# A graph network on one core: target rows copied into PSUM by ScalarE in the edge stages, and stationary weights in the first mixture of experts

## The chip, the cores and the metric

The kernel runs on one core of a Trainium2 chip, as one program. The metric is the time on the device in microseconds (us), lower is better. TensorE does matmuls, VectorE and ScalarE work on SBUF and PSUM, GpSimd here does little but issue indirect DMAs (gathers and scatters by index), and SyncE issues the other DMAs.

## The reference, cut to what matters

Four layers are computed over 625 nodes with 768 features. Only the first one is touched by the change. It is a graph layer over 20000 edges (source, target), and behind it a mixture of eight experts of which each token takes two.

```python
def gatv2(x, src, dst, Ws, bs, Wd, bd, attn):            # called twice: 8 heads of 96, 1 head of 768
    fs = (x @ Ws + bs).reshape(-1, H, D)
    fd = (x @ Wd + bd).reshape(-1, H, D)
    e = jax.nn.leaky_relu(fs[src] + fd[dst], 0.2)
    logits = jnp.einsum('ehd,hd->eh', e, attn)
    m = jax.ops.segment_max(logits, dst, num_segments=N)
    ex = jnp.exp(logits - m[dst])
    ...
    out = jax.ops.segment_sum(alpha[:, :, None] * fs[src], dst, num_segments=N)
# mixture: two experts of eight per token, E = 8, D = 768, F = 3072
#   y = gelu(x @ w1[e] + b1[e]) @ w2[e] + b2[e], mixed by the gates
```

## The kernel before, in words

**Two edge stages.** Two tables of 625 rows (776 floats each: 768 features and 8 linear terms) are written to HBM, one for source nodes and one for target nodes. The 20000 edges are 157 tiles of 128. For each tile GpSimd issues a gather of 128 source rows (L538), a gather of 128 target rows (L541) and, six tiles behind, a scatter of the tile's logits (L549). All go in this one order on GpSimd, and a scatter starts only when the scatter before it has landed (`s_sc`). There are eight buffers for each table's rows. VectorE does the arithmetic: it adds the two rows (L1254, 776 columns), takes the maximum with zero and multiplies by the attention vector (first stage L1258; second stage L1268, which sums as well), in the first stage sums each head (L1263), and finishes the logit (L1275). In the first stage it also makes two one-hot rows of 626 bf16 columns for each tile (L1206), with which TensorE counts edges into PSUM banks 0 to 6 (L611), and SyncE clears two tables in HBM beside it, one transfer behind every third scatter. ScalarE has nothing to do in either stage. GpSimd's order and these waits set the pace:

```python
for i in range(ET + LAG):          # ET = 157 tiles, LAG = 6
    if i < ET:
        gathers(i)                 # L538, L541
    ...
    if i >= LAG:
        scatter(i - LAG, g)        # L549: waits s_lg (logits ready) and s_sc (last scatter landed)
```

**The first mixture** works on units of 256 token slots, each with one expert's weights, 8 units here. A unit has 12 groups `g` of 256 hidden features. Fp32 accuracy comes from fp32r matmuls of a rounded part and a rest: every product is three matmuls, (high, high), (high, low), (low, high). `first(u, g)` makes the hidden features from weights as the stationary operand and token columns as the moving one; it has 36 matmuls of `columns` columns. `second(u, g)` makes the output with tokens stationary and weights moving; it has 12 matmuls of 384 columns for each 128 tokens, into banks 4 to 7. Both are at L780. `columns` is 128, 192 or 256, by how far the unit is filled (`empty`). TensorE's order is first(g + 1), second(g), then the next unit's rows are transposed (`turn`, L773), second(11) and the next unit's first(0), behind which stands the branch of the unit loop. ScalarE rounds weights (L1038, L1043) and applies Gelu (L1050); VectorE makes the rests of the weights (L1555, L1560), splits the hidden features (L1566, L1568), and copies the output out of PSUM (L1585) when second(11) is done, from where GpSimd stores it (L584).

## Time and profile before

| | |
|---|---|
| time, median of 3 runs | 4110.46 us (4107.86 to 4110.98) |
| the profiled execution's own time | 4104.76 us |
| its span | 4103.0 us |
| TensorE, weight loads, VectorE, ScalarE, GpSimd busy | 60%, 49%, 53%, 19%, 28% |
| mean granted TensorE clock | 0.763 of full speed |

The times come from the device; the profile is one execution, taken apart by engine. In it a line such as L549 is a line of the kernel. A group of instructions has its busy time and the mean of one. A timeline row has the start, the duration, the engine and, in brackets, how long the engine was idle before it and what ended that. A window row has its ends and length, the busy time of PE, PEld (weight loads), DVE, ACT and POOL, with the number of instructions as (x...), then the granted TensorE clock as a share of full speed, the DMA share and GB/s.

### The profile page before, as it was taken

To read this page: it belongs to the slowest core of one execution; us is meant where nothing else is said; L and a number is where in the kernel's file an instruction comes from. 1 tells how busy PE (TensorE), PEld (TensorE's weight loads), DVE (VectorE), ACT (ScalarE), POOL (GpSimd) and SP (SyncE) were. 2 spreads that over 40 slices of the span, in tenths; PEclk is the share of its full clock that TensorE was granted. 3 is DMA by queue.
4 is the path that set the end of the run, shared out by engine and by line. 5 is a ranking of instruction groups with operands and counts; after the bars stand their busy time and mean duration, and the time that the engine had idled before them with its cause. 6 is when DMAs were issued, how large, how long until landed. Compare 5 with 4: busy or idle time off the path is not lost.

```text
span 4103.0 us, 37498 instructions
## 1 busy us (share of the span) xinstructions
PE 2477.2 (60%) x13152; PEld 2028.0 (49%) x13153; DVE 2179.4 (53%) x3944; ACT 769.6 (19%) x1107; POOL 1132.9 (28%) x987
## 2 busy tenths in 40 slices
PE   8445555556600000015599888888588487886899
PEld 4333343345300000003599888888275244475799
DVE  3666677767444444434575455545474524567332
ACT  0000000024000000001364334433072111044110
POOL 0667677730277777750100000000100000000000
PEclk9666655667855555556799999999788687998799
DMA  8666666653365666640675555554300001100111
GB/s 261 198 206 212 213 178 178 172 136 115 99 174 173 176 177 178 179 116 1 196 265 194 171 177 177 179 170 148 114 1 12 10 27 36 58 12 24 70 70 42
DMA packets 117558, 543.01 MB, mean 132 GB/s; under 512 B 31195, under 2 KB 31451, under 8 KB 112220
## 3 DMA queue, kind: packets, MB, share of 16 engines
q0 software_dynamic: 65920, 264.29, 22.1%
q1 hardware_dynamic: 50088, 262.32, 19.0%
q10 hardware_dynamic: 1386, 14.06, 1.1%
q8 instruction: 121, 1.98, 0.2%
q14 instruction: 43, 0.35, 0.0%
HBM read 486.31 MB, written 54.26 MB: 132 GB/s over the span
## 4 chain that ended last, share of the span: by engine, by line
PE 43%; issue 31%; POOL 9%; DMA 8%; DVE 8%; ACT 1%; SPq 0%; POOLq 0%; DVEq 0%; ACTq 0%
PE PS L780 18%; PE PS L642 7%; PE PS L873 6%; DMA logits<-lgr,key 6%; PE PS L697 4%; POOL logits L549 3%; POOL WB L538 3%; POOL WB L541 2%; PE PS L683 1%; PE PS L750 1%; PE PS L854 1%; PE PS L740 1%; DVE stats L1181 1%; PE PS L626 1%; DVE W L1343 1%
## 5 line engine op out<-in xcount | busy, mean ns | idle before, releaser
L611 PE MATMUL PS<-O 128*125 128x512 bf16 (+9 forms) x1727 | 404.9, 410 | 355.5 <-DVE O L1206 344.3
L683 PE MATMUL PS<-ident,W 125*125 125x125 f32 x650 | 113.7, 313 | 811.7 <-issue 737.8
L1254 DVE TENSOR_TENSOR WB<-WB 128x776 f32<-128x776 f32 x276 | 267.4, 969 | 561.9 <-DMA WB<-dst_rows,idx 558.4
L611 PEld LDWEIGHTS PS<-O 128*125 128x125 bf16 x1727 | 275.3, 200 | 485.2 <-DVE O L1206 404.5
L683 PEld LDWEIGHTS PS<-ident,W 125*125 125x125 f32 x650 | 96.1, 215 | 827.0 <-issue 771.9
L780 PE MATMUL PS<-urowsT,w1s 128*128 128x192 f32 (+2 forms) x3492 | 430.4, 283 | 73.2 <-issue 65.6
L549 POOL DMA_INDIRECT logits<-lgr,key x314 | 416.3, 1326 | 210.9 <-DMA logits<-lgr,key 118.8
L780 PEld LDWEIGHTS PS<-urowsT,w1s 128*128 128x128 f32 x3492 | 428.4, 199 | 75.5 <-issue 71.1
L538 POOL DMA_INDIRECT WB<-src_rows,idx x314 | 321.2, 1023 | 293.8 <-DMA dst_rows<-O 198.7
L642 PE MATMUL PS<-WB,XT 128*125 128x384 f32 (+1 forms) x1120 | 377.5, 500 | 13.8 <-DMA WB<-in_L_gnn_Wos 12.6
L780 PE MATMUL PS<-w2s,hid 128*128 128x384 f32 x2016 | 369.0, 336 | 5.3 <-issue 5.3
L780 PEld LDWEIGHTS PS<-w2s,hid 128*128 128x128 f32 x2016 | 346.5, 188 | 6.1 <-issue 6.1
L541 POOL DMA_INDIRECT WB<-dst_rows,idx x276 | 309.2, 1120 | 84.7 <-issue 74.9
L531 POOL TENSOR_TENSOR rstd<-var,mhalf 125x5 f32<-125x5 f32 x13 | 15.3, 1174 | 1117.9 <-DVE var L1186 1071.5
L697 PE MATMUL PS<-F,PT 125*125 125x96 f32 (+3 forms) x1500 | 294.2, 349 | 9.8 <-DVE O L1367 9.5
L642 PEld LDWEIGHTS PS<-WB,XT 128*125 128x125 f32 x1120 | 210.7, 189 | 177.3 <-issue 30.6
L999 ACT ACTIVATE W<-W,nmx 125x625 f32<-125x625 f32 x130 | 106.1, 816 | 881.0 <-DVE nmx L1345 878.1
L873 PE MATMUL PS<-w3s,XT 128*128 128x384 f32 x1440 | 255.4, 340 | 11.1 <-DVE w3s L1617 11.1
L873 PEld LDWEIGHTS PS<-w3s,XT 128*128 128x128 f32 x1440 | 255.1, 190 | 12.3 <-issue 12.2
L697 PEld LDWEIGHTS PS<-F,PT 125*125 125x125 f32 x1500 | 232.5, 204 | 51.4 <-issue 16.2
L584 POOL DMA_DIRECT2D slot_outs<-F x8 | 5.8, 729 | 871.7 <-DVE F L1585 871.7
L1560 DVE TENSOR_TENSOR w2s<-PB,w2s 128x1536 fp32r<-128x1536 f32 x97 | 170.4, 1757 | 132.6 <-ACT w2s L1043 132.6
(224 smaller groups left out, 3186.8 us busy)
## 6 DMA issues: line engine op xcount, KB each, us to landing
XN<-in_L_ffn_w SPq DMA_DIRECT2D x98, 769.0 KB, 4.4
PB<-in_L_ffn_w SPq DMA_DIRECT2D x97, 768.0 KB, 5.0
logits<-NEG ACTq DMA_DIRECT2D x9, 1367.2 KB
WB<-logits SPq DMA_DIRECT2D x5, 2187.5 KB
slot_rows<-NEG SPq DMA_DIRECT2D x13, 768.0 KB
slot_outs<-NEG SPq DMA_DIRECT2D x12, 768.0 KB
C<-in_L_ffn_expert_w SPq DMA_DIRECT2D x8, 1152.0 KB, 5.5
NEG<-in_L_ffn_expert_w SPq DMA_DIRECT2D x8, 1152.0 KB, 6.5
```

The source lines that it names most:

```text
L538: pool.indirect_dma_start(out=gs[u], out_offset=None, in_=src_rows, in_offset=bass.IndirectOffsetOnAxis(ap=idx[:, i, 0:1], axis=0)).then_i ...
L541: pool.indirect_dma_start(out=gd[u], out_offset=None, in_=dst_rows, in_offset=bass.IndirectOffsetOnAxis(ap=idx[:, i, 1:2], axis=0)).then_i ...
L549: pool.indirect_dma_start(out=tables[g], out_offset=bass.IndirectOffsetOnAxis(ap=key[:, i:i + 1], axis=0), in_=lgr[:, i % EU, 0:HEADS[g][" ...
L611: mm = pe.matmul(PSz[0:R, a:b], oh[:, slot, 1, c * R:(c + 1) * R], oh[:, slot, 0, a - c * N:b - c * N], start=(first and fresh), stop=last ...
L642: mm = pe.matmul(PS[0:R, 4 + g % 4, 0:hw], XT[:, k, t * R:(t + 1) * R], w[:, k, half * hw:(half + 1) * hw], start=(k == 0), stop=(k == kc ...
L683: tr = pe.transpose(PSz[0:R, 1024 * (1 + s % 2) + b * P:1024 * (1 + s % 2) + b * P + R], src[:, b * R:(b + 1) * R], ident[0:R, 0:R])
L697: mm = pe.matmul(PS[0:R, bank, 0:cw], PT[0:R, s % 2, b, :], F[0:R, b, col:col + cw], start=(b == 0), stop=(b == T - 1))
L780: mm = pe.matmul(out, w(i), x(j), start=first and n == 0, stop=last and n == 2)
L873: mm = pe.matmul(PS[:, 4 + 2 * ((MB3 + d) % 2) + half, 0:384], XT2[:, a, k, t * R:t * R + P], w3s[:, 2 * u + k // 3, b, col:col + 384], st ...
L999: act.activation(W[0:R, v % 4, :], W[0:R, v % 4, :], ACT.Exp, bias=nmx[:, v % 4:v % 4 + 1], accum_out=den[:, v % 4:v % 4 + 1]).then_inc(s_ ...
L1254: dve.tensor_tensor(gs[u], gs[u], gd[u], ALU.add).then_inc(s_z, 1)
L1560: dve.tensor_tensor(w2s[:, g % 2, 1, :], uw2[g % 2], w2s[:, g % 2, 0, :].bitcast(F32), ALU.subtract).then_inc(s_lo2, 1)
```

## The change

In the edge stages ScalarE copies the target rows into PSUM, so that VectorE adds SBUF and PSUM. In the first stage PSUM has one bank free (bank 7), so the row goes in two halves of 384 columns through `zh`; in the second stage whole rows go through four areas `zw`. The source one-hot is made by ScalarE in two activations (Abs of the gap, Relu of one minus it).

```diff
+        zh = PS[:, 7, 0:D // 2]
+        zw = [PSz[:, 1024 * b:1024 * b + GW] for b in range(4)]
...
+            def edges(g):
...
+                def half_copy(i, u, half):
+                    wait(act, s_mul, 2 * i + half)
+                    act.copy(zh, gd[u][:, half * (D // 2):(half + 1) * (D // 2)]).then_inc(s_gc, 1)
...
+                def step(i, u, rounds):
+                    gathered(u, rounds)
+                    if g == 0:
+                        half_copy(i, u, 0)
+                        node_gaps(i)
+                        half_copy(i, u, 1)
+                        source_onehot(i, u)
+                    else:
+                        wait(act, s_lg, ET + i - 3)
+                        act.copy(zw[u % 4], gd[u]).then_inc(s_gc, 1)
...
-                def add(i, u, rounds):
-
-                    dve.wait_ge(s_gat[u], rounds + 32 * (ER + (u < ET % EU)) * g + 32)
-                    dve.tensor_tensor(gs[u], gs[u], gd[u], ALU.add).then_inc(s_z, 1)
-
-                def product(i, u):
-                    dve.wait_ge(s_z, i + 1)
-                    dve.scalar_tensor_tensor(out=gs[u][:, 0:D], in0=gs[u][:, 0:D], scalar=0.0, in1=attn, op0=ALU.max,
-                                             op1=ALU.mult).then_inc(s_mul, 1)
+                def half_product(i, u, half):
+                    part = slice(half * (D // 2), (half + 1) * (D // 2))
+                    dve.wait_ge(s_gc, 2 * i + half + 1)
+                    dve.tensor_tensor(zh, gs[u][:, part], zh, ALU.add).then_inc(s_z, 1)
+                    dve.wait_ge(s_z, 2 * i + half + 1)
+                    dve.scalar_tensor_tensor(out=gs[u][:, part], in0=zh, scalar=0.0, in1=attn[:, part],
+                                             op0=ALU.max, op1=ALU.mult).then_inc(s_mul, 1)
...
+                def add(i, u):
+                    dve.wait_ge(s_gc, 2 * ET + i + 1)
+                    dve.tensor_tensor(zw[u % 4], gs[u], zw[u % 4], ALU.add).then_inc(s_z, 1)
```

VectorE, first edge stage, one tile. Before:

```order
L1275 SCALAR_TENSOR_TENSOR lgr<-dots,WB 128x8
L1254 TENSOR_TENSOR WB<-WB 128x776
L1257 REGISTER_ALU
L1258 SCALAR_TENSOR_TENSOR WB<-WB,PB 128x768
L1206 ISA
L1206 TENSOR_SCALAR O<-XT,idf 128x626
L1263 TENSOR_REDUCE dots<-WB 128x8
L1206 ISA
L1206 TENSOR_SCALAR O<-XT,idf 128x626
```

and with the change (the lines are those of the changed kernel; L1338 is the add, L1340 the product, L1345 the add of the linear terms):

```order
L1338 TENSOR_TENSOR PS<-WB,PS 128x384
L1340 SCALAR_TENSOR_TENSOR WB<-PS,PB 128x384
L1291 ISA
L1291 TENSOR_SCALAR O<-XT,idf 128x626
L1337 REGISTER_ALU
L1338 TENSOR_TENSOR PS<-WB,PS 128x384
L1340 SCALAR_TENSOR_TENSOR WB<-PS,PB 128x384
L1345 TENSOR_TENSOR WB<-WB 128x8
L1349 TENSOR_REDUCE dots<-WB 128x8
```

One one-hot and the wide add are gone, the add and the product stand twice at half the width, and the second half stands behind a copy of ScalarE.

In the mixture the high and low parts of the moving operand go through one matmul (`both`, two runs of `columns` side by side in a bank), so each high weight tile is loaded once. `second` has the weights stationary too and the hidden features moving, so the output comes out transposed, in banks 2 to 7, and is turned back by TensorE (`turn_back`) at the unit's end. The small part, in the second half of a bank, is added by ScalarE and VectorE: ScalarE copies it out with the bias, VectorE adds the large part, ScalarE applies Gelu.

```diff
-                def three(out, w, x, first, last):
-
-                    for n, (i, j) in enumerate(((0, 0), (0, 1), (1, 0))):
-                        mm = pe.matmul(out, w(i), x(j), start=first and n == 0, stop=last and n == 2)
-                    return mm
+                def both(bank, columns):
+
+                    return PS[:, bank, :].rearrange("p (j n) -> p j n", j=2)[:, :, 0:columns]
...
+                            pe.matmul(both(q % 2, columns), w1s[:, g % 2, 0, w:w + P],
+                                      urowsT2[:, :, k * TU:k * TU + columns], start=k == 0, stop=False)
+                            mm = pe.matmul(PS[:, q % 2, 0:columns], w1s[:, g % 2, 1, w:w + P],
+                                           urowsT2[:, 0, k * TU:k * TU + columns], start=False, stop=k == KD - 1)
...
+                    for c in range(FC):
+                        pe.wait_ge(s_hl, (u * NG + g) * FC + c + 1)
+                        for k in range(KD):
+                            w = c * D + k * P
+                            pe.matmul(both(2 + k, columns), w2s[:, g % 2, 0, w:w + P],
+                                      hid2[:, g % 2, :, c * TU:c * TU + columns],
+                                      start=g == 0 and c == 0, stop=False)
+                            mm = pe.matmul(PS[:, 2 + k, 0:columns], w2s[:, g % 2, 1, w:w + P],
+                                           hid2[:, g % 2, 0, c * TU:c * TU + columns],
+                                           start=False, stop=g == NG - 1 and c == FC - 1)
...
                     for g in range(NG - 1):
                         first(u, g + 1, columns)
-                        second(u, g, -(-columns // P))
-                    turn(u + 1)
+                        second(u, g, columns)
+                    turn(u + 1, (0, 1))
+                    second(u, NG - 1, columns)
...
+                    turn(u + 1, (2,))
                     first(u + 1, 0)
+                    turn_back(u)
...
+                def sum_hidden(u, g):
+                    for c in range(FC):
+                        q = g * FC + c
+                        part = hid[:, g % 2, c * TU:(c + 1) * TU]
+                        dve.wait_ge(s_un, u * (NG * FC) + q + 1)
+                        dve.tensor_tensor(part, PS[:, q % 2, 0:TU], part, ALU.add).then_inc(s_ha, 1)
```

TensorE, one group of a unit with 192 columns. Before (first, then second):

```order
L780 MATMUL PS<-urowsT,w1s 128x192 x36
L780 MATMUL PS<-w2s,hid 128x384 x24
```

and with the change, for a unit with 128 columns, the last pair of first and the first two pairs of second (`first` has 12 such pairs, `second` too; w1s and w2s are the weights):

```order
L808 MATMUL PS<-urowsT,w1s 128x2x128
L810 MATMUL PS<-urowsT,w1s 128x128
L823 MATMUL PS<-hid,w2s 128x2x128
L826 MATMUL PS<-hid,w2s 128x128
L823 MATMUL PS<-hid,w2s 128x2x128
L826 MATMUL PS<-hid,w2s 128x128
```

A group goes from 60 matmuls (48 in a unit of 128 columns) to 48, and both halves of it now depend on `columns`.

## Rows read from the trace of the kernel before

**Rows 1.** Windows: both edge stages, a unit of 128 columns, a later unit
```profile
108.00:880.00 772.00, 404.87 (x1727) 275.31 (x1727) 539.58 (x946) 4.09 (x2) 547.94 (x471) 0.63 0.62 188
1096.00:1834.00 738.00, 0.15 (x2) 0.16 (x1) 306.69 (x640) 1.08 (x3) 539.73 (x471) 0.50 0.60 172
...
2085.00:2162.00 77.00, 75.19 (x588) 74.87 (x588) 59.05 (x66) 46.80 (x51) 0.80 (x1) 1.00 0.79 268
...
2292.00:2409.00 117.00, 105.28 (x732) 105.01 (x732) 59.99 (x65) 46.84 (x51) 0.71 (x1) 0.95 0.53 176
```

**Rows 2.** Windows of the scatters alone (L549)
```profile
130.00:525.00 395.00, 95.94 (x79) 0.65 0.66 208
525.00:878.00 353.00, 106.46 (x79) 0.62 0.57 164
1121.00:1820.00 699.00, 212.31 (x156) 0.50 0.60 172
```

**Rows 3.** Second edge stage: the scatters' group
```profile
L549 POOL DMA_INDIRECT logits<-lgr,key x157 | 213.3, 1358 | 84.7 <-DMA logits<-lgr,key 41.4 <-issue 29.6 <-DVE lgr L1275 13.7
```

**Rows 4.** Second edge stage: timeline of GpSimd and VectorE
```profile
1443.08 0.97 DVE L1254 TENSOR_TENSOR WB<-WB 128x776 f32<-128x776 f32 x1 [2.00 <-DMA WB<-dst_rows,idx]
1443.44 1.42 POOL L541 DMA_INDIRECT WB<-dst_rows,idx  x1 [0.30 <-DMA logits<-lgr,key]
...
1445.17 0.99 POOL L549 DMA_INDIRECT logits<-lgr,key  x1 [0.30 <-DVE lgr L1275]
...
1449.60 1.45 POOL L549 DMA_INDIRECT logits<-lgr,key  x1 [0.92 <-DMA logits<-lgr,key]
...
1472.03 0.98 POOL L549 DMA_INDIRECT logits<-lgr,key  x1 [0.80 <-DMA logits<-lgr,key]
...
1475.85 1.67 POOL L549 DMA_INDIRECT logits<-lgr,key  x1 [0.30 <-issue]
```

**Rows 5.** First edge stage: timeline, a sum per head beside a scatter
```profile
606.80 0.94 DVE L1263 TENSOR_REDUCE dots<-WB 128x8 f32<-128x768 f32 x1
606.85 0.99 POOL L549 DMA_INDIRECT logits<-lgr,key  x1 [0.30 <-issue]
```

**Rows 6.** Groups of VectorE and ScalarE that price the new instructions
```profile
L1263 DVE TENSOR_REDUCE dots<-WB 128x8 f32<-128x768 f32 x157 | 148.0, 943 | 0.0
...
L1235 DVE TENSOR_TENSOR O<-PS,PB 125x384 f32<-125x384 f32 x20 | 11.1, 557 | 46.1 <-PE PS L642 46.1
...
L1555 DVE TENSOR_TENSOR w1s<-XN,w1s 128x1536 fp32r<-128x1536 f32 x98 | 171.6, 1751 | 0.0
L1050 ACT ACTIVATE F<-PS,b1c 128x256 f32<-128x256 f32 x192 | 91.0, 474 | 305.6 <-PE PS L780 305.6
L1568 DVE TENSOR_TENSOR hid<-F,hid 128x512 fp32r<-128x512 f32 x96 | 66.5, 693 | 3.3
```

**Rows 7.** Mixture: timeline, a hand-over from ScalarE to VectorE
```profile
2379.65 1.48 ACT L1043 CAST w2s<-PB 128x1536 fp32r<-128x1536 f32 x1 [2.32 <-PE PS L780]
2381.16 1.76 DVE L1560 TENSOR_TENSOR w2s<-PB,w2s 128x1536 fp32r<-128x1536 f32 x1 [1.88 <-ACT w2s L1043]
```

**Rows 8.** Mixture: groups of TensorE by shape
```profile
L780 PE MATMUL PS<-w2s,hid 128*128 128x384 f32 x2016 | 369.0, 336 | 5.3 <-issue 5.3
L780 PE MATMUL PS<-urowsT,w1s 128*128 128x192 f32 x1584 | 194.4, 283 | 42.1 <-issue 42.1
...
L780 PE MATMUL PS<-urowsT,w1s 128*128 128x256 f32 x1116 | 145.4, 291 | 31.1 <-issue 23.5 <-DVE w1s L1555 3.9 <-DVE urowsT L1548 3.7
...
L780 PE MATMUL PS<-urowsT,w1s 128*128 128x128 f32 x792 | 90.9, 274 | 0.0
```

**Rows 9.** Mixture: timeline at the end of a unit, and of the last one
```profile
2393.43 4.48 PE L780 MATMUL PS<-urowsT,w1s 128*128 128x256 f32 x36
...
2409.87 3.52 PE L780 MATMUL PS<-urowsT,w1s 128*128 128x192 f32 x15 [11.97 <-issue]
...
2858.52 1.82 DVE L1585 COPY F<-PS 128x768 f32<-128x768 f32 x2 [1.83 <-PE PS L780]
```

More of the change, by code:

```diff
@@ L801, in second, with turn_back @@
                         wait(pe, s_uy, u * SU)
[L802 to L810 removed]
+                    for c in range(FC):
[8 more added lines that the diff above has]
+                                           start=False, stop=g == NG - 1 and c == FC - 1)
+                    mm.then_inc(s_ub, 1)
+                def turn_back(u):
+                    for half in range(2):
+                        pe.wait_ge(s_ya, u * 2 + half + 1)
+                        for s in range(SU):
+                            for k in range(KD // 2):
+                                tr = pe.transpose(PS[:, 2 + 3 * half + s, k * P:(k + 1) * P],
+                                                  yT[:, half * (KD // 2) + k, s * P:(s + 1) * P], ident[:])
+                        tr.then_inc(s_yt, 1)
                 def groups(u, columns):
@@ L825, in unit @@
                         groups(u, TU // 2)
-                        second(u, NG - 1, SU // 2)
                     with pe.Else():
@@ L1049, in hidden, with output_part @@
                         act.wait_ge(s_ua, u * (NG * FC) + q + 1)
-                        act.activation(hid[:, g % 2, c * TU:(c + 1) * TU], PS[:, q % 4, 0:TU], ACT.Gelu,
-                                       bias=b1c[:, g % 2, c:c + 1]).then_inc(s_ug, 1)
+                        act.activation(hid[:, g % 2, c * TU:(c + 1) * TU], PS[:, q % 2, TU:2 * TU], ACT.Identity,
+                                       bias=b1c[:, g % 2, c:c + 1]).then_inc(s_un, 1)
+                def hidden(u, g):
+                    for c in range(FC):
+                        part = hid[:, g % 2, c * TU:(c + 1) * TU]
+                        act.wait_ge(s_ha, u * (NG * FC) + g * FC + c + 1)
+                        act.activation(part, part, ACT.Gelu).then_inc(s_ug, 1)
+                def output_part(u):
+                    act.wait_ge(s_ub, u * NG + NG)
+                    for half in range(2):
+                        wait(act, s_yt, u * 2 + half - 1)
+                        act.copy(yT[:, 3 * half:3 * half + 3, :], PS[:, 2 + 3 * half:5 + 3 * half, TU:2 * TU])\
+                           .then_inc(s_yb, 1)
                 def unit(u):
                     for g in range(NG):
+                        if g:
+                            small_part(u, g)
                         hidden(u, g)
@@ L1290, in step @@
                     else:
+                        add(i, u)
                         if lag:
@@ L1596, in mixture0 @@
                         unit(u)
-                dve.wait_ge(s_ua, units * (NG * FC) + FC)
+                dve.wait_ge(s_yt, units * 2)
                 dve.nop().then_inc(s_left, 1)
```

157 lines of the change are left out of this document (99 added, 58 removed).

## The prediction, made before the changed kernel was run

> **What bounds the kernel now.** I read the windows of the stages first, because the change touches two kinds of stage with different limits. The two edge stages take 772 and 738 us, the mixture's units 77 us each where they have 128 columns and about 117 us otherwise [rows 1]. In the second edge stage TensorE and ScalarE do nothing, VectorE is busy 307 of 738 us and GpSimd 540. So the chain there is GpSimd's: two gathers and a scatter a tile. The windows of the scatters give the pace: 156 scatters in 699 us are 4.48 us a tile in the second stage; in the first, 79 in 395 us are 5.00 us while SyncE clears tables, and 79 in 353 us are 4.47 us after that [rows 2].
>
> Next I looked at what makes GpSimd's own instructions long. The scatters of the second stage take 1.36 us on the mean [rows 3], but 0.99 where nothing disturbs them [rows 4]. In the timeline, a gather that started at 1443.44, while VectorE's add of two SBUF rows (from 1443.08 to 1444.05) ran, took 1.42 us and ended 0.81 us after that add [rows 4]. The 1.45 and the 1.67 in the same rows are of that kind too. So an issue that comes while VectorE reads two SBUF rows waits for the end of that. A head sum that ran beside a scatter, with one SBUF input, left it at 0.99 [rows 5]. The page "SBUF — State Buffer" of the Trainium skill, section "Who interferes with whom", has this as a rule: a VectorE instruction with two SBUF inputs keeps a GpSimd instruction that reads SBUF waiting, one with a single SBUF input outside the two-port modes does not. By that rule, which the 1.42 and the 0.99 bear out, the changed add and product disturb nobody.
>
> What is left without the stretch? Two undisturbed scatters, each followed by two undisturbed gathers, show the next scatter 4.43 us behind (1445.17 to 1449.60, the last one having waited 0.92 for the landing of the one before) and 3.82 us behind (1472.03 to 1475.85, no wait) [rows 4]. The lower one is GpSimd's pure issue time, the upper one is set by the scatter's way through the DMA queue behind two gathers.
>
> In the mixture TensorE bounds: 105 of 117 us are busy, and 12 us are one hole behind the next unit's first group, ended by nothing that the profile shows, where the unit's branch stands [rows 1, 9]. The kernel before has its matmuls at 0.130 us each for 256 columns (145.4 / 1116), 0.123 for 192, 0.115 for 128 and 0.183 for 384 [rows 8]. From 128 to 192 columns nothing is gained or lost, so there the weight load sets the pace, and above it the columns do. The counts say which units there are: 1584 matmuls of 192 columns are 4 units (11 groups of 36), 792 of 128 are 2, and the remaining 2 are full.
>
> **Second edge stage.** ScalarE's copy of 776 columns (about 0.85 us, between 0.47 for 256 and 1.48 for 1536 [rows 6, 7]) lies beside GpSimd's 4 us and four areas let it run ahead: nothing. VectorE's add and product stay at 0.97 and 0.95. GpSimd's tile goes from 4.48 to between 3.82 and 4.43. I take the middle, 4.12, as the DMA queue still has the same bytes: 0.36 x 156 = **56 us** gained (ends 8 and 103).
>
> **First edge stage.** VectorE now has a chain with ScalarE in it, since both halves go through one bank. A half is add and product at 384 columns with PSUM: 0.557 each by the nearest row [rows 6]. Two SBUF rows, 0.693 for 512 columns and 1.751 for 1536, give 1.033 ns a column and 0.164 fixed [rows 6]; at that slope the PSUM row has 0.557 - 0.397 = 0.160 fixed: no price for PSUM. "VectorE: DVE Perf Modes" of the Trainium skill, section "The TRN2 errata", gives 120 cycles of fixed cost for PSUM sources against 58 for SBUF, which would add about 0.06 us to each of four, 0.26 us a tile, and bring the stage's gain to about nothing; the rows disagree with it, and the sum goes by them. Between the halves stands ScalarE's copy of 384 columns, 0.57 (0.474 for 256, and 0.78 ns a column more [rows 6, 7]); the target one-hot lies beside it. The chain is 4 x 0.557 + 0.57 + head sum 0.94 + two small ones at 0.16 = 4.06, and some five hand-overs at 0.03 (2381.13 to 2381.16 [rows 7]) = 4.2 us. The copy of the next tile's first half lies beside the head sum. ScalarE has two copies and two activations of 626 columns, about 2.7 us, and TensorE's counting waits for nobody longer than before. So VectorE at 4.2 and GpSimd at 4.12 are about even, and I take 4.25. After the clearing: 0.22 x 79 = 17 us. During it, one scatter in three waits for SyncE's transfer, which the change leaves; of the others' stretch I count 0.2 x 79 = 15 us. Together **32 us** gained (ends: 84 gained with 3.9 us a tile after the clearing and 4.5 during it; 50 lost if the hand-overs are 0.2 each, 5.06 us a tile).
>
> **Mixture, groups.** The slope from 256 to 384 columns gives 0.236 for 512. A group half is 12 pairs: 12 x (0.236 + 0.130) = 4.39 us in a full unit, against 36 x 0.130 = 4.69 for first and 24 x 0.183 = 4.39 for second; 12 x (0.183 + 0.123) = 3.67 with 192 columns, against 4.42 and 4.39; 12 x (0.130 + 0.115) = 2.94 with 128, against 4.13 and 2.20. With 11 firsts and 12 seconds: a 192 unit gains 8.2 + 8.6 = 16.9, a full one 3.3, and each one 0.3 for the next unit's first(0).
>
> VectorE gets more in each group: rests of both weights 1.75 + 1.76 [rows 6, 7], two sums of 256 columns from PSUM at 0.42, four smaller splits, 1.42; with the wait for Gelu (0.47) and for ScalarE's rounding behind it, I make it 6.4 to 6.5 us a group, whatever the columns. That is below the 7.3 us of a 192 group, but above the 5.9 of a 128 group: the two small units become VectorE's, 12 x 6.5 = 78 us and some 5 for the unit's end, against 77 now: 12 us lost in the two.
>
> **Mixture, unit ends.** The third pair of row blocks is now turned only behind second(11), and then ScalarE (0.59) and VectorE (0.68, by the 512-column row [rows 6]) have to pass before the next first(0): 1.4 us of idle TensorE. turn_back is 12 transposes, 1.5 us. The hole of 12 us stays, as the branch does [rows 9]. So 2.9 us lost a unit: 192 units net 14.3 x 4 = 57, full ones 0.7 x 2 = 1. After the last unit the output was copied out right behind second(11) [rows 9]; now first(8, 0) (4.4), the turned rows and the turning back stand ahead: 7 us lost on the path. Larger memsets ahead of the mixture lie before the wait for scattered token rows: nothing (3 us if that cover were gone). Sum of the mixture: 57 + 1 - 12 - 7 = **39 us** gained (ends: 75 gained if small units stay TensorE's and unit ends cost nothing, 20 lost if the longer chain shows in each group).
>
> **The sum.** 56 + 32 + 39 = 127. The profiled execution took 4104.8 us, 5.7 below the median, so it would take 3978; against the median, 3983. I say 3980.
>
> **The rivals.** (a) *The issue stays stretched*, because the stretch hangs on the product or on fp32 work as such and not on a second SBUF input. For it speaks that no row shows GpSimd beside an instruction that reads PSUM; against it the 1.42 beside an add and the 0.99 beside a head sum [rows 4, 5]. Both edge stages then gain nothing: 4110 - 39 = 4071. The Trainium skill leans to it in one place: the same section of "SBUF — State Buffer" infers that making descriptors needs only the write side, so that an add of two SBUF rows would not hold it up. Chance 0.09. (b) *The landing gives way too.* Without stretches the queue runs evenly and tiles go at 3.85: 42 us more in the second stage, and with small units at 77 another 12 or so: 3925. Rows that wait 0.8 to 0.9 for landings speak against it. Chance 0.13. (c) *The mixture's longer chain shows.* PSUM, Gelu and sums go round ScalarE, VectorE, ScalarE, VectorE in each group, with weights rounded in between; at 8 us a group the mixture gains nothing: 4022 to 4045. Chance 0.10. (d) *Slower: the first edge stage becomes a ping-pong of two engines.* Its one bank makes ScalarE and VectorE wait for each other six times a tile. The chain is 4.06 us without hand-overs, and the stage's tile now takes (395 + 353) / 158 = 4.73 [rows 2]. It eats the 95 us of the other two when a tile costs 0.6 more, 5.3 us, that is with hand-overs of 0.25 us and more. At 6 us a tile it loses 200: 4110 - 95 + 200 = 4215. For it: the order on ScalarE puts an activation between the copies. Against: 0.03 in the row. Chance 0.05.
>
> **How the numbers follow.** The forecast has 0.63, from 3950 to 4020 by its own ends. A measurement of this kernel tells about 0.2%, 8 us, from no change. To hold 8 in 10, the range takes (b)'s middle and most of (c): 3925 to 4055, leaving out (a), (d) and the outer part of (b). Faster by over 0.2%: all but (d) and a rest, 0.94; within it 0.02; slower 0.04.
>
> **What would show it.** Scatters and gathers near 0.99 and 0.95 us, 4.1 us a tile in the second stage and 4.2 to 4.3 in the first; VectorE's adds near 0.56; pairs of matmuls that sum to 0.31 us with 192 columns, units of 192 near 103 us, of 128 near 83; the hole of 12 us at each unit's end. Scatters still at 1.36 say (a), idle VectorE behind ScalarE's copies says (d), idle TensorE inside groups says (c).

## The result, and the profile after

The changed kernel takes **3962.91 us** (median of 4 runs, 3955.41 to 3966.71), the kernel before in the same comparison 4109.16 (4101.91 to 4110.98): a ratio of **0.9645, 95% interval 0.9626 to 0.9664**. A second comparison gave 3961.46 against 4105.06, 0.9650 (0.9632 to 0.9667). So 146 us went (predicted: 130), and the predicted 3980 is 17 us too high. The copy of the change in that second comparison had a span of 3955.4 us in its trace, 10 us under the one read here.

| | before | after | predicted gain | gain |
|---|---|---|---|---|
| profiled span, us | 4103.0 | 3965.0 | 127 | 138 |
| first edge stage, start of the first gather to start of the last scatter | 769.1 | 715.1 | 32 | 54 |
| second edge stage | 718.8 | 666.2 | 56 | 53 |
| mixture, first transpose of rows to the next layer's norm | 895.7 | 865.9 | 39 | 30 |
| the rest | 1719.4 | 1717.8 | 0 | 2 |

(The rest is the span less the three rows above.) That the sum came near is in part luck: two terms were off in opposite directions, by 22 and by 9 us. The windows of the changed kernel, of the first and the second edge stage, of a unit with 192 columns, a full one and a small one (span, then busy time and count of TensorE, weight loads, VectorE, ScalarE, GpSimd, then the granted clock, DMA share and GB/s):

```profile
109.00:824.50 715.50, 371.25 (x1727) 256.32 (x1727) 569.39 (x1260) 391.74 (x631) 457.87 (x471) 0.69 0.66 203
1050.00:1716.00 666.00, 0.00 (x0) 0.00 (x0) 299.26 (x628) 127.01 (x157) 454.25 (x471) 0.50 0.66 188
2080.30:2183.40 103.10, 89.33 (x601) 87.86 (x601) 72.90 (x116) 57.24 (x77) 0.72 (x1) 0.93 0.63 215
2183.40:2303.00 119.60, 106.14 (x600) 92.05 (x600) 72.82 (x115) 57.46 (x77) 0.71 (x1) 0.96 0.50 173
1901.50:1984.70 83.20, 75.31 (x589) 72.92 (x589) 71.73 (x115) 55.68 (x79) 0.00 (x0) 0.95 0.67 229
```

Against [rows 1], GpSimd is busy for 458 instead of 548 us in the first stage and for 454 instead of 540 in the second, for the same 471 instructions. A 192-column unit fell from about 117 to 103 us, the two small ones rose from 78.4 and 77.1 to 83.1 and 82.5, and a full one rose from 117.3 to 119.6. The windows of the scatters alone, during the clearing, after it, and in the second stage:

```profile
126.00:520.00 394.00, 81.65 (x81) 0.65 0.67 215
520.00:824.00 304.00, 74.95 (x75) 0.75 0.64 184
1068.00:1716.00 648.00, 153.18 (x157) 0.50 0.65 185
```

That is 4.86, 4.05 and 4.13 us a tile, where [rows 2] has 5.00, 4.47 and 4.48. And the groups of the second edge stage's GpSimd instructions (scatter, gather of source rows, gather of target rows), where [rows 3] has 1358 ns for the scatter:

```profile
L562 POOL DMA_INDIRECT logits<-lgr,key x157 | 154.7, 985 | 113.4 <-DMA logits<-lgr,key 79.8 <-issue 31.7 <-DVE lgr L1368 1.9
L551 POOL DMA_INDIRECT WB<-src_rows,idx x157 | 152.2, 969 | 157.3 <-DMA dst_rows<-O 109.8 <-issue 47.5
L554 POOL DMA_INDIRECT WB<-dst_rows,idx x138 | 130.5, 946 | 44.5 <-issue 40.5 <-DMA logits<-lgr,key 4.0
```

No instruction of this stage is stretched any more (0.99 us at most once the pipeline is full, where 131 of 457 took more than 1.05 before), and the largest wait before the scatter is now the landing of the scatter before it (79.8 us; 41.4 before). The timeline of GpSimd and VectorE answers to [rows 4]:

```profile
1438.86 0.97 DVE L1354 TENSOR_TENSOR PS<-WB,PS 128x776 f32<-128x776 f32 x1 [1.78 <-ACT PS L1020]
1439.64 0.99 POOL L562 DMA_INDIRECT logits<-lgr,key  x1 [0.30 <-issue]
...
1442.21 0.95 POOL L554 DMA_INDIRECT XT<-dst_rows,idx  x1 [0.30 <-issue]
1443.46 0.99 POOL L562 DMA_INDIRECT logits<-lgr,key  x1 [0.31 <-issue]
...
1443.46 0.97 DVE L1354 TENSOR_TENSOR PS<-WB,PS 128x776 f32<-128x776 f32 x1 [2.69 <-ACT PS L1020]
...
1447.90 0.99 POOL L562 DMA_INDIRECT logits<-lgr,key  x1 [0.92 <-DMA logits<-lgr,key]
```

At 1443.46 an add and a scatter start together, and the scatter takes its 0.99 us. From there to the scatter at 1447.90 are 4.44 us, 0.92 of them a wait for the landing; the one before came 3.82 us apart, with no wait. These are the prediction's two ends.

### The profile page after: what moved, and what is told of

It reads as the page before. It is cut to its first block, busy times and chain, and to the rows that moved or that the text cites. A ratio compares the mean times of both kernels' runs of the same rounds, so it can differ in the third digit from the quotient of the medians.

```text
span 3965.0 us, 39470 instructions
## 1 busy us (share of the span) xinstructions
PE 2387.2 (60%) x12372; PEld 1917.4 (48%) x12373; DVE 2312.3 (58%) x4660; ACT 1360.7 (34%) x2102; POOL 960.6 (24%) x987
## 4 chain that ended last, share of the span: by engine, by line
PE 40%; issue 30%; DMA 11%; DVE 11%; POOL 4%; ACT 3%; DVEq 0%; SPq 0%; POOLq 0%; ACTq 0%
PE PS L656 8%; DMA logits<-lgr,key 7%; PE PS L903 6%; PE PS L808 5%; PE PS L823 4%; PE PS L711 4%; PE PS L810 2%; DMA WB<-dst_rows,idx 2%; PE PS L826 2%; POOL WB L551 1%; PE PS L697 1%; POOL logits L562 1%; PE PS L764 1%; DVE w1s L1645 1%; PE PS L884 1%
## 5 line engine op out<-in xcount | busy, mean ns | idle before, releaser
L808 PE MATMUL PS<-urowsT,w1s 128*128 128x384 f32 (+2 forms) x1164 | 375.7, 386 | 85.1 <-issue 64.3
L562 POOL DMA_INDIRECT logits<-lgr,key x314 | 313.7, 999 | 273.8 <-DMA logits<-lgr,key 196.0
L1354 DVE TENSOR_TENSOR PS<-WB,PS 128x776 f32<-128x776 f32 x157 | 152.4, 971 | 358.4 <-ACT PS L1020 358.4
L823 PE MATMUL PS<-hid,w2s 128*128 128x384 f32 (+2 forms) x1152 | 338.8, 362 | 0.5 <-DVE hid L1668 0.5
L810 PE MATMUL PS<-urowsT,w1s 128*128 128x192 f32 (+2 forms) x1164 | 306.1, 263 | 0.0
L1020 ACT COPY PS<-WB 128x776 f32<-128x776 f32 x138 | 111.6, 809 | 561.3 <-DMA WB<-dst_rows,idx 561.3
L826 PE MATMUL PS<-hid,w2s 128*128 128x192 f32 (+2 forms) x1152 | 288.9, 251 | 0.0
L808 PEld LDWEIGHTS PS<-urowsT,w1s 128*128 128x128 f32 x1164 | 232.2, 200 | 109.4 <-issue 82.0
L1000 ACT COPY PS<-WB 128x384 f32<-128x384 f32 x276 | 133.2, 483 | 358.4 <-DMA WB<-dst_rows,idx 263.3
L1338 DVE TENSOR_TENSOR PS<-WB,PS 128x384 f32<-128x384 f32 x314 | 176.2, 561 | 135.5 <-ACT PS L1000 134.4
```

The lines of the kernel that those rows point to most:

```text
L562: pool.indirect_dma_start(out=tables[g], out_offset=bass.IndirectOffsetOnAxis(ap=key[:, i:i + 1], axis=0), in_=lgr[:, i % EU, 0:HEADS[g][" ...
L808: pe.matmul(both(q % 2, columns), w1s[:, g % 2, 0, w:w + P], urowsT2[:, :, k * TU:k * TU + columns], start=k == 0, stop=False)
L810: mm = pe.matmul(PS[:, q % 2, 0:columns], w1s[:, g % 2, 1, w:w + P], urowsT2[:, 0, k * TU:k * TU + columns], start=False, stop=k == KD - 1)
L823: pe.matmul(both(2 + k, columns), w2s[:, g % 2, 0, w:w + P], hid2[:, g % 2, :, c * TU:c * TU + columns], start=g == 0 and c == 0, stop=False)
L826: mm = pe.matmul(PS[:, 2 + k, 0:columns], w2s[:, g % 2, 1, w:w + P], hid2[:, g % 2, 0, c * TU:c * TU + columns], start=False, stop=g == NG ...
```

## The experiments

Twelve runs in four comparisons, each on a chip of its own, with the kernel before beside them (4105.31, 4105.06, 4106.49 and 4105.78 us). First the parts alone, and the two halves of the SBUF question.

**The edges alone.** The change, with the mixture's functions and memsets of the kernel before.

```diff
-                dve.memset(PS[:, 0:2, :], 0.0)
-                link(dve.memset(PS[:, 2:8, :], 0.0))
+                dve.memset(PS[:, 3, 0:TU], 0.0)
+                link(dve.memset(PS[:, 6:8, 0:384], 0.0))
...
-                def both(bank, columns):
+                def three(out, w, x, first, last):
```

> The edge stages of the change with the mixture of before. If the two parts are independent, this keeps what the two edge stages gained in the profile of the change (from the first source gather to the last scatter: 769.1 to 715.0 us and 718.8 to 666.2 us) and nothing else: near 4002 us. If part of the measured gain came from the mixture helping elsewhere (clock, code loading), it would lie outside 3994 to 4012.

Measured: 4059.79, ratio 0.9888 (0.9869 to 0.9907). A miss by 58 us. The second stage gained as it should (671.8 us), but the first took 768.7.

**The mixture alone.** The reverse: the kernel before with the change's mixture.

```diff
-                def three(out, w, x, first, last):
+                def both(bank, columns):
```

> The mixture of the change with the edge stages of before. Independent parts: 4104 - 30 = near 4075 us, units of 192 columns 103 us from one first matmul to the next, small ones 82 us. If the mixture's gain needed the new edge stages, near 4104.

Measured: 4063.96, ratio 0.9898 (0.9879 to 0.9917): 41 us gained, where 30 were forecast. The mixture took 857.3 us in its trace and the 192 units that can be read 100.4 to 102.7, so this copy of it ran 3 to 9 us faster than in the two traces of the change.

**Copies into SBUF.** The four areas of the second stage lie in SBUF, so that the add and the product read two SBUF rows again, and all else stays.

```diff
-        zw = [PSz[:, 1024 * b:1024 * b + GW] for b in range(4)]
+        zw = [XTz[:, (b + 1) * GW:(b + 2) * GW] for b in range(4)]
```

> The change, but in the second edge stage ScalarE copies the target rows into SBUF instead of PSUM; the same copies, waits and order. Theory (a second SBUF input of VectorE holds GpSimd up): scatters back near 1.36 us and a tile near 4.48 us, the stage 50 us longer, the kernel near 4013 us, with the first edge stage as in the change. Rival (the gain comes from ScalarE taking part, from timing, or from the four areas that let VectorE start apart from the gather): scatters stay at 0.99 us, the kernel at 3963 us.

Measured: 4061.38, ratio 0.9896 (0.9875 to 0.9918). The theory's 4013 was missed by 48 us: its first stage too took 769.2 us. The second took 706.7, 35 more than in the edges alone beside it.

**The product from SBUF.** The add reads PSUM but writes its sum to SBUF, so that the product alone has two SBUF inputs.

```diff
-                    dve.tensor_tensor(zw[u % 4], gs[u], zw[u % 4], ALU.add).then_inc(s_z, 1)
+                    dve.tensor_tensor(gs[u], gs[u], zw[u % 4], ALU.add).then_inc(s_z, 1)
...
-                    dve.scalar_tensor_tensor(out=gs[u][:, 0:D], in0=zw[u % 4][:, 0:D], scalar=0.0, in1=attn,
+                    dve.scalar_tensor_tensor(out=gs[u][:, 0:D], in0=gs[u][:, 0:D], scalar=0.0, in1=attn,
```

> The change, but in the second edge stage only the add reads PSUM: it writes its sum to SBUF, and the product reads two SBUF inputs as before. If every VectorE instruction with two SBUF inputs holds GpSimd up for its length, half of the stretch comes back: scatters of 1.15 to 1.25 us, a tile near 4.3 us, the kernel near 3985 us. If the product is what does it all, as most long scatters of before stood beside it: near 4013 us. If it is the add alone: 3963 us.

Measured: 4042.31, ratio 0.9846 (0.9826 to 0.9866). First stage 771.2, second 689.5, 18 more than in the edges alone; without the 56 us of the first stage this is near the 3985 of "half of the stretch".

These three have the first stage of the change line for line, and it took 54 us more than in the change. Where does it stand? In the timeline of the edges alone, TensorE, its weight loads, ScalarE and VectorE:

```profile
706.14 2.90 PE L625 MATMUL PS<-O 128*125 128x512 bf16 x11 [0.92 <-issue]
...
714.19 0.82 ACT L993 ACTIVATE O<-XT,ones 128x626 bf16<-128x626 bf16 x1 [5.11 <-remote]
714.24 0.39 DVE L1257 TENSOR_SCALAR O<-XT,idf 128x626 bf16<-128x626 f16 x1 [5.68 <-remote]
```

ScalarE's and VectorE's one-hots wait for a buffer that TensorE's counting frees. Its matmuls are issued at 706.14, but in the semaphore's records no count comes until 714.1, and from about tile 83 on this happens at every fifth tile: five tiles in 24.5 us instead of 20.4. The question was whether that belongs to these kernels.

**The change again.** No edit.

> The changed kernel, unchanged, once more. Its own trace has 715 us from the first gather of the first edge stage to its last scatter; in the three runs of kernels whose code for that stage is the same (edges alone, SBUF areas, product from SBUF) it took 769 to 771 us, with a stop of 4 us at every fifth tile from tile 83 on, in which VectorE, ScalarE and TensorE all stand. If the stop hangs on something outside the code (the chip or the moment), this run shows it too: about 4018 us. If it belongs to those kernels (where their code or their buffers lie), this run has none: 3963 us, first stage 715 us.

Measured, on a second chip: 3961.46, ratio 0.9650 (0.9632 to 0.9667), first stage 715.5.

**One waiter.** The source one-hot waits behind the target one-hot instead of on TensorE.

```diff
-                    wait(act, s_ohu, i - 1)
+                    act.wait_ge(s_oh, i + 1)
```

> ScalarE's source one-hot no longer waits on the semaphore that TensorE counts up (one-hots used) but on VectorE's target one-hot of the same tile, which has waited on it. If the stops of every fifth tile come from two engines that wait on one semaphore of TensorE, they go: first stage 715 us whatever the run of the unchanged copy beside it shows. If they have another cause, the time is within 8 us of that copy.

Measured: 3963.99, ratio 0.9649 (0.9629 to 0.9669). On this chip the copy had no stops either, so it tells nothing of them.

**The edges alone again**, and **copies into SBUF again**, on a third chip.

> The edges alone once more, unchanged. If the stops of every fifth tile in the first edge stage hang on something outside the code, they are absent or present here as in the other two kernels beside it, whose first stage has the same code: without them 4005 us (first stage 715 us), with them 4060 us (769 us). If they belong to this kernel alone, this run has them and the narrow gather has not.

Measured: 3993.80, ratio 0.9722 (0.9700 to 0.9745), first stage 713.3, second 660.7, mixture 897.8.

> The copies of the second edge stage in SBUF once more, unchanged. First stage as in the two kernels beside it if the stops come from outside the code: then 4004 us without them, of which the second stage's stretched descriptors are 41 us over the change; with them 4061 us.

Measured: 4004.15, ratio 0.9748 (0.9727 to 0.9769), first stage 713.5, second 706.1.

So the stops are not in the code: the same two kernels ran 66 and 57 us faster on the third chip. Whether they hung on the first chip or on the hour, these runs can't tell. The windows of the scatters in the first stage, edges alone on the first chip and on the third:

```profile
560.00:820.00 260.00, 52.25 (x53) 0.68 0.56 164
```

```profile
560.00:820.00 260.00, 64.88 (x65) 0.74 0.64 183
```

Free of the stops, the SBUF pair gives a clear answer: with the copies in SBUF the second stage takes 45 us more than with the copies in PSUM (706.1 against 660.7, same chip), 40 us more than in the trace of the change. Its GpSimd groups, and behind them those of the product from SBUF:

```profile
L562 POOL DMA_INDIRECT logits<-lgr,key x157 | 197.3, 1257 | 78.1 <-issue 47.6 <-DMA logits<-lgr,key 28.2 <-DVE lgr L1368 2.4
L551 POOL DMA_INDIRECT WB<-src_rows,idx x157 | 186.3, 1186 | 157.8 <-DMA dst_rows<-O 110.3 <-issue 47.5
L554 POOL DMA_INDIRECT WB<-dst_rows,idx x138 | 131.1, 950 | 42.4 <-issue 39.9 <-DMA logits<-lgr,key 2.4
```

```profile
L551 POOL DMA_INDIRECT WB<-src_rows,idx x157 | 187.4, 1193 | 157.0 <-DMA dst_rows<-O 109.5 <-issue 47.5
L562 POOL DMA_INDIRECT logits<-lgr,key x156 | 156.0, 1000 | 98.8 <-DMA logits<-lgr,key 60.0 <-issue 35.9 <-DVE lgr L1368 2.9
```

With two SBUF inputs in both, scatter and source gather take 0.27 and 0.22 us more than in the change. With them in the product alone, only the source gather (which falls beside it) is stretched, the scatter is not (1.00 us, where 1.15 to 1.25 were forecast), and the stage costs 18 us more than the edges alone on that chip (689.5 against 671.8). So both of VectorE's instructions, the add and the product, stretch an issue that they meet. That the row is copied and that the work is fp32 play no part, since both stayed. Rival (a) falls. The rule in "SBUF — State Buffer" of the Trainium skill, section "Who interferes with whom", agrees with that. The same section's inference that making descriptors needs only the write side would leave these issues at their length, and they grew by 0.2 us; since they also read their indices from SBUF, the runs don't say which part of an issue waits.

In the first edge stage the copy wasn't moved to SBUF. Its scatters after the clearing fell from 1.33 us on the mean to 1.00, so the same cause is likely there, but only the second stage shows it.

Next, what sets the edge stages now.

**The source one-hot back on VectorE.**

```diff
-                        node_gaps(i)
                         half_copy(i, u, 1)
-                        source_onehot(i, u)
...
+                dve.tensor_scalar(oh[:, slot, 0, :], iota16, idf[:, 0, bass.ds(i, 1)], None, ALU.is_equal)
```

> The source one-hot of the first edge stage goes back to VectorE, and ScalarE only copies. If VectorE sets the tile (its instructions sum to about 3.9 us of 4.1 in the trace of the change), its 0.38 us more come on top: 157 x 0.38 = 60 us over the copy of the change in the same comparison. If the chain over ScalarE (two copies of 0.48 us and two activations of 0.81 us, which stand between the copies) sets it, the copies come sooner and the time is the same or up to 40 us less.

Measured: 3965.84, ratio 0.9656 (0.9638 to 0.9675), 4.4 us over the copy of the change beside it, and not 60; the two intervals overlap. The windows of all engines in the first stage, the copy of the change and this kernel:

```profile
560.00:820.00 260.00, 130.04 (x680) 90.85 (x678) 227.19 (x495) 154.95 (x247) 177.74 (x184) 0.77 0.64 184
```

```profile
560.00:820.00 260.00, 131.31 (x672) 90.36 (x671) 241.62 (x555) 62.33 (x124) 178.96 (x183) 0.76 0.64 184
```

VectorE's busy share went from 87 to 93% and ScalarE's from 60 to 24%, and GpSimd issued as much as before. Neither VectorE nor the chain through ScalarE sets the tile.

**Less traffic.** The gather of the target rows fetches 194 of 776 columns in the second stage.

```diff
-                    out=gd[u], out_offset=None, in_=dst_rows,
+                    out=gd[u] if g == 0 else gd[u][:, 0:194], out_offset=None,
+                    in_=dst_rows if g == 0 else dst_rows.rearrange("n d -> (n d)")[0:N * 194].rearrange("(n d) -> n d", n=N),
...
-                        act.copy(zw[u % 4], gd[u]).then_inc(s_gc, 1)
+                        act.copy(zw[u % 4].rearrange('p (k n) -> p k n', n=194),
+                                 gd[u][:, 0:194].unsqueeze(1).to_broadcast([P, 4, 194])).then_inc(s_gc, 1)
```

> In the second edge stage the gather of the target rows fetches 194 of 776 columns, and ScalarE writes these four times side by side into the same PSUM area, so that every engine has as many instructions of the same size as in the change, and only the traffic falls (from 6.2 to 3.9 KB per edge); the scores of that stage are computed from part of the target row. If the tile (4.15 us in the change) is the scatter's issue until it has landed (3.3 us from its start) and 0.85 us until the next starts, a scatter with less traffic ahead of it lands sooner and the tile falls to what GpSimd's three instructions and their pauses take, 0.97 + 0.95 + 0.99 + 3 x 0.30 = 3.8 us: 157 x 0.35 = 55 us off the second stage, 3908 us. If GpSimd or the chain over VectorE and ScalarE sets it, the second stage stays at 660 to 666 us and the time at 3963 us.

Measured: 3928.34, ratio 0.9560 (0.9538 to 0.9581). The second stage took 609.4 us, 57 less than in the trace of the change (the forecast had 55); the mixture, whose units depend on the scores, had a 192 unit in place of a small one and took 890.3 us instead of 865.0 in the copies into SBUF beside it, so the total isn't comparable (3908 was forecast). The windows of 570 us of scatters of the second stage, in the copy of the change and here, then the scatters' group here:

```profile
1130.00:1700.00 570.00, 136.04 (x138) 0.50 0.66 190
```

```profile
1080.00:1650.00 570.00, 147.92 (x150) 0.50 0.47 128
```

```profile
L563 POOL DMA_INDIRECT logits<-lgr,key x157 | 154.9, 987 | 58.8 <-issue 46.6 <-DMA logits<-lgr,key 10.1 <-DVE lgr L1370 2.2
```

That is 4.13 and 3.80 us a tile. The instructions are the same, the wait before the scatter that a landing ended fell from 79.8 to 10.1 us, and the tile is GpSimd's own time, 2.90 us of issue and three pauses of 0.30. So with full rows the scatter's landing is the limit.

The first stage of this kernel is that of the change, and its trace holds the landings. It settles what sets the pace there, where the profile puts most waits before a scatter down to VectorE's logits (27.3 of 44 us between 560 and 820 us of the change). Of 66 scatters after the clearing (tiles 85 to 150), 49 wait longer than the usual 0.30 us. All 49 start 0.77 to 0.79 us behind the landing of the scatter before, and the logits of such a tile are ready more than 12 us before its scatter. A scatter lands 3.30 us (median) behind its start, and 3.30 + 0.77 = 4.07 us is the tile of that stage (4.10). With the narrow rows the landing comes 2.28 us behind the start, and the next scatter 1.5 us later.

Shortening it at full traffic, with two scatters in flight, wasn't tried: two scatters may write the same row, and their order would be open.

Last, the ends of the units.

**Turn back first.** TensorE turns the output back ahead of the next unit's first product.

```diff
-                    first(u + 1, 0)
                     turn_back(u)
+                    first(u + 1, 0)
```

> At the end of each mixture unit TensorE turns the output of the unit back before it multiplies the first rows of the next unit, where the change does it after. Where the change idles twice there (1.48 us before the next unit's first product and 1.1 to 1.7 us before the turn back), one of the two would be hidden: 8 units x 1.1 to 1.5 = 9 to 12 us under the copy of the change. If VectorE, whose work for the two stands in one order, sets both, the one wait only moves: within 4 us of the copy.

Measured: 3974.93, ratio 0.9681 (0.9666 to 0.9696), so 13.5 us slower than the copy beside it. A miss of both theories, and a premise was wrong: in the change TensorE has no idle time before the turn back. The 1.1 to 1.7 us that the expectation puts there stand before the turn of the third pair of row blocks (L790), at the ends of all units but the full ones, and they stay here. In the change at the end of a 192 unit and of a full one, and then here at the end of the same full one:

```profile
2386.67 0.65 PE L790 MATMUL PS<-ident,F 128*128 128x128 f32 x4 [1.10 <-DVE urowsT L1638]
...
2285.28 0.49 PE L808 MATMUL PS<-urowsT,w1s 128*128 128x512 f32 x1 [1.48 <-DVE urowsT L1638]
```

```profile
2291.23 2.41 PE L837 MATMUL PS<-ident,XT 128*128 128x128 f32 x12 [2.37 <-DVE XT L1675]
2293.29 0.78 PE L808 MATMUL PS<-urowsT,w1s 128*128 128x512 f32 x1
```

The wait for the output's two sums is 2.37 us where that for the turned rows was 1.48; in the change the first product (4.3 us) hides it. Also, the transposes behind the longer gap take 2.41 instead of 1.47 us and the first products 0.78 instead of 0.49. The granted clock is 0.66 in these transposes, and 1.00 in the change's. The longer wait and the transposes come to some 16 us over eight ends; the six holes are 2.5 us shorter in sum (15.1 and 15.8 us before the full units, 8.2 to 8.5 before three 192 units), which leaves 13 us, near the 13.5 between the medians (the two traces lie 19 us apart). Why the holes shift so is open.

**The loop over units written out.** On TensorE alone.

```diff
-                with pe.Fori(1, NU) as u:
-                    with pe.If(u < units):
-                        unit(u)
+                def rest(u):
+                    if u < NU:
+                        with pe.If(units > u):
+                            unit(u)
+                            rest(u + 1)
+
+                rest(1)
```

> TensorE's loop over the mixture units is written out (each further unit inside the condition of the one before), so that its sequencer no longer jumps back between units; the three sizes of a unit and all other engines' loops stay. In the trace of the change the idle time before the first product of a unit in the loop is 5.84, 10.84, 11.99, 10.93, 11.86 and 11.41 us, and in it the sequencer shows two long branches, the jump back (5.8 to 7.2 us, of which some 5 lie behind TensorE's last work) and the jump over the small unit's code (5.2 to 5.9 us). If the jump back is what it waits for, six gaps fall by about 5 us each, to 6 to 7 us: 30 us, 3933 us. If the sequencer waits for code whichever way it gets there, or if another engine's loop is as late, the gaps stay at 11 to 12 us and the time within 5 us of 3963.

Measured: **3938.69** (3933.56 to 3941.15), ratio 0.9594 (0.9580 to 0.9608): faster than both kernels, 23 to 24 us under the two medians of the change, on another chip. The mixture took 841.9 us (865.9 and 860.2 in the two traces of the change). The gap before a full unit, and before one with 192 columns, in the change and here:

```profile
2183.39 0.79 PE L808 MATMUL PS<-urowsT,w1s 128*128 128x512 f32 x1 [10.84 <-issue]
...
2303.01 0.68 PE L808 MATMUL PS<-urowsT,w1s 128*128 128x384 f32 x1 [11.99 <-issue]
```

```profile
2181.34 0.77 PE L808 MATMUL PS<-urowsT,w1s 128*128 128x512 f32 x1 [9.70 <-issue]
...
2294.43 0.66 PE L808 MATMUL PS<-urowsT,w1s 128*128 128x384 f32 x1 [4.96 <-DVE w1s L1650]
```

The six gaps sum to 62.9 us in the change and to 39.7 here: 23 us, which is the gain. 21 of them came from three gaps before 192 units, which fell to 4.6 to 5.0 us and are now ended by VectorE's split of the weights. Before a full unit little changed (9.7 and 10.1 us). There the sequencer's records show a jump over the small unit's code of 6.3 us and one over the 192 unit's of 4.9, where the change has 5.8 for the jump back, 5.2 and 0.25. So the first theory holds for one kind of unit and the second for the other. (At the first of the six, before a 192 unit too, the gap was already 5.84 us and fell to 5.42.)

## Why the prediction was right, and where it was wrong

**The stretch (right).** Scatters at 0.985 and gathers at 0.969 and 0.946 us, as forecast; undone by moving the copies to SBUF, with 40 to 45 us of stage time. VectorE's add from PSUM takes 0.971 at 776 columns as before, and 561 ns at 384, where the estimate from the slope was 557:

```profile
L1338 DVE TENSOR_TENSOR PS<-WB,PS 128x384 f32<-128x384 f32 x314 | 176.2, 561 | 135.5 <-ACT PS L1000 134.4
```

The page "VectorE: DVE Perf Modes" of the Trainium skill, section "The TRN2 errata", would have 0.06 us more for a PSUM source; this row has none.

**Second edge stage (right, with luck in the number).** 4.12 us a tile was forecast, 4.13 measured, 53 us gained of 56. I took the middle between a tile that waits for the landing (4.43) and one that doesn't (3.82) without a reason for the middle; the timeline shows why it was close: for long stretches the two alternate. Rival (b), that the landing gives way, needed less traffic, as the narrow gather shows, and the change has the same.

**First edge stage (the term was mis-sized: 54 instead of 32).** The step that failed is the chain of 4.2 us on VectorE and ScalarE, by which "I take 4.25". After the clearing it is 4.05. Two things were off. The chain is shorter than the 4.2: hand-overs between dependent instructions cost the 0.03 us that I took, but an instruction that doesn't depend on the one ahead starts 0.04 to 0.08 us before that one's recorded end; here the turn of one tile, from its first add to its last small instruction:

```profile
701.83 0.56 DVE L1338 TENSOR_TENSOR PS<-WB,PS 128x384 f32<-128x384 f32 x1
...
702.42 0.56 DVE L1340 SCALAR_TENSOR_TENSOR WB<-PS,PB 128x384 f32<-128x384 f32 x1
...
703.01 0.48 ACT L1000 COPY PS<-WB 128x384 f32<-128x384 f32 x1 [0.57 <-DVE WB L1340]
...
703.52 0.56 DVE L1338 TENSOR_TENSOR PS<-WB,PS 128x384 f32<-128x384 f32 x1 [0.25 <-ACT PS L1000]
704.12 0.56 DVE L1340 SCALAR_TENSOR_TENSOR WB<-PS,PB 128x384 f32<-128x384 f32 x1
...
704.60 0.16 DVE L1345 TENSOR_TENSOR WB<-WB 128x8 f32<-128x8 f32 x1
704.72 0.95 DVE L1349 TENSOR_REDUCE dots<-WB 128x8 f32<-128x768 f32 x1
...
705.59 0.16 DVE L1368 SCALAR_TENSOR_TENSOR lgr<-dots,WB 128x8 f32<-128x8 f32 x1
```

3.76 us until the last small one starts, 3.92 with it, where I had 4.2; and the copy took 0.48, not 0.57. And so it isn't the bound at all: with 0.38 us more on VectorE the tile stays (one-hot back on VectorE), and the first stage of the narrow gather shows what the bound is, the scatter's landing, as in the second stage. By the starts of the scatters, the first 80 tiles (most of them during the clearing) took 403.4 us before and 389.9 after, 14 gained against 15 forecast, and the other 76 took 343.5 and 307.4, 36 gained against 17; the last 4 us lie before the first scatter. Rival (d), a ping-pong of two engines, is refuted on the same rows: ScalarE's copy starts 0.03 us behind the product that frees the bank.

**Mixture (30 instead of 39).** The same mixture took 857.3 to 867.1 us in the eight traces that have its units unchanged, and the old one 895.7 to 897.8 in three, so 29 to 40 us were gained, and the profile read here lies at the low end. The 192 units gained 12.6 us each (14.3 forecast; 117.2, 115.8 and 116.6 to 103.1, 102.5 and 105.9). The term that failed is "a full one 3.3": full units lost 2.4 and 3.5 us. Their prices came from groups over all units, [rows 8], and these mix in the matmuls behind the hole, where the granted clock is low. In the timeline of the kernel before, the 36 matmuls of `first` and the 24 of `second` in the middle of a full unit, and a `first` of a 192 unit right behind the hole and in its middle, with the windows of both stretches (the granted clock is 0.54 of full speed in the one and 1.00 in the other):

```profile
2311.66 4.47 PE L780 MATMUL PS<-urowsT,w1s 128*128 128x256 f32 x36
2315.97 4.33 PE L780 MATMUL PS<-w2s,hid 128*128 128x384 f32 x24
2320.14 4.47 PE L780 MATMUL PS<-urowsT,w1s 128*128 128x256 f32 x36
...
2409.87 7.48 PE L780 MATMUL PS<-urowsT,w1s 128*128 128x192 f32 x36 [11.97 <-issue]
...
2429.60 4.16 PE L780 MATMUL PS<-urowsT,w1s 128*128 128x192 f32 x36
```

```profile
2409.90:2417.30 7.40, 7.40 (x37) 7.40 (x38) 0.00 (x0) 0.47 (x1) 0.00 (x0) 0.54 0.02 6
2429.00:2434.00 5.00, 5.00 (x44) 5.00 (x43) 2.06 (x2) 2.17 (x3) 0.00 (x0) 1.00 0.50 158
```

From 2311.66 to 2320.14 a group of a full unit took 8.48 us, not the 9.08 that I worked out (4.69 + 4.39). In the change a group takes (from the start of one `second` to the next):

```profile
2197.60 0.40 PE L823 MATMUL PS<-hid,w2s 128*128 128x512 f32 x1
...
2206.08 0.40 PE L823 MATMUL PS<-hid,w2s 128*128 128x512 f32 x1
```

8.48 again (8.32 in the second full unit): full units gain next to nothing in a group, and lose the unit's end (2.9 us forecast). The same mistake did less harm for 192 columns, where before and after were too dear nearly alike (8.19 instead of 8.81, 6.83 instead of 7.34): a group gains 1.36 us instead of 1.47, some 1.2 us a unit.

**Small units (right sum, by two errors).** They lost 4.7 and 5.4 us, and 6 was forecast. VectorE does set their pace, as forecast (in most groups TensorE waits 0.25 to 0.28 us for its sum of the hidden features, L1658), but at 6.02 us a group and not 6.5, hardly less than the 6.11 before. The rest of such a unit takes 10 to 11 us, where I had 5.

**The unit's end and the hole (right)**: 1.48 us of idle TensorE before the next first product and 1.47 for the transposes. The 192 units have another 1.1 to 1.5 us of idle time before the turn of the third pair, which takes the place of 1.1 to 1.6 us within their last `second` in the kernel before. The hole is 11 to 12 us (5.84 at the first of the six). Rival (c) didn't come: in the full unit from 2183 to 2303 TensorE has no gap but the 1.48 and the hole.

**The parts together.** The edges alone gained 112.7 us (third chip), the mixture alone 41.4 (first chip), together 154 against 144 to 146. The 8 to 10 us between are at the limit of what these runs can tell, across chips.

## What to carry to other kernels

A GpSimd issue that runs beside VectorE work with two SBUF inputs is worth a copy into PSUM by an idle engine, even if it doubles VectorE's instructions: here the tiles fell by 0.35 to 0.42 us, and moving the copy alone back to SBUF cost 0.29. Take durations for a sum from the middle of a steady stretch, since means over a whole kernel hold the slow stretches behind idle time; and take chains from start to start, not as a sum of durations. Where the profile names a releaser for a wait on two semaphores, look up whether that one had long been done: here it was VectorE, done for 12 us, and the landing was what ended the wait. And before a new chain is made the bound, price what remains of the old one: here the scatter's landing, at 4.1 us, hid the whole chain.

## What the runs showed of the hardware

- **In one comparison, on one chip, three kernels had stops that no other had.** Two kernels ran there at 4059.79 and 4061.38 us and on another chip at 3993.80 and 4004.15. In all three kernels with the new first edge stage TensorE's counts came late at every fifth tile: in the edges alone ScalarE waited 59.4 us in 14 times for them between 560 and 870 us. In the stretch from 696 to 728 us TensorE's granted clock was 0.50 throughout (the mean over 560 to 820 is 0.68, and 0.74 on the other chip). The kernel before and the mixture alone show nothing of the kind there: 4105.31 us for the kernel before on that chip, 4105.06 to 4109.16 elsewhere, and a first stage of 765.7 us in the trace of the mixture alone. The cause stays open, and chip and hour weren't told apart. The changed kernel itself wasn't run on that chip; by these three I estimate 4018 us there.
- **A hole costs TensorE more than its length.** Behind the 12 us the 36 matmuls of a 192 unit took 7.48 us instead of 4.16, 3.3 us more, at a granted clock of 0.54 instead of 1.00; in the change the 24 of the same place took 6.4 instead of 3.4, at 0.50 instead of 1.00.
- **Most long jumps of TensorE's sequencer take 3.3 to 7.7 us**, whether back to the loop's start or over a branch's code. Not all do: the jump over the 192 unit's code takes 0.25 us before a full unit in the change, and 4.9 and 5.7 with the loop written out. VectorE's jumps back at the same places take 0.06 to 0.08; its loop has some 115 instructions a unit where TensorE has 600 matmuls.
